# A fused attention, feed-forward and recurrence kernel: roots of the last group norms on ScalarE, an output bias part formed ahead, a third bank for the last receptance, last steps on VectorE, and a rearranged first attention

## The reference

```python
# layer 0
x = x + attention(qkv(layernorm(x)), self_mask) @ w_ao + b_ao          # 16 heads of 16
x = x + attention(q(layernorm(x)), kv(encoder), cross_mask) @ w_co + b_co
x = x + gelu(layernorm(x) @ w1 + b1) @ w2 + b2
# layer 1
xn = layernorm(x); sx = previous_token(xn) - xn
x5 = xn + sx * (maa_stack + tanh((xn + sx * maa_x) @ maa_w1) @ maa_w2)  # five mixes
w = exp(-exp(time_decay + tanh(x5[1] @ decay_w1) @ decay_w2))
r, k, v, g = x5[3] @ Wr.T, x5[0] @ Wk.T, x5[2] @ Wv.T, silu(x5[4] @ Wg.T)
for t: out = r_t . (u * k_t v_t + s); s = k_t v_t + w_t * s             # 32 heads of 8
att = group_norm(out, 32 groups of 8) * gn_w + gn_b
x = x + (att * g) @ Wo.T
xn2 = layernorm(x); sx2 = previous_token(xn2) - xn2
rr = sigmoid((xn2 + sx2 * ffn_maa_r) @ ffn_Wr.T)
kk = relu((xn2 + sx2 * ffn_maa_k) @ ffn_Wk.T) ** 2
x = x + rr * (kk @ ffn_Wv.T)
```

## Time and profile before

| | |
|---|---|
| median of 3 runs | 695.53 us (695.42 to 696.07) |
| profiled execution | 695.38 us, span 693.6 us, mean granted TensorE clock 0.985 |
| TensorE busy | 645.6 us (93%) |
| VectorE busy | 597.0 us (86%) |
| ScalarE busy | 570.5 us (82%) |
| GpSimd busy | 314.9 us (45%) |
| chain that ended last | TensorE 71%, ScalarE 13%, VectorE 8%, issue 5%, GpSimd 2% |

### The profile page before, as it was taken

One profiled execution on the slowest core, in us unless ns is written; L12 is line 12 of the kernel. 1 busy time (PEld: TensorE's weight loads), 2 busy tenths in 40 slices (PEclk: granted clock), 3 DMA queues, 4 the chain that ended last, 5 costly groups with the idle time before them and its releaser, 6 DMA issues.

```text
span 693.6 us, 17394 instructions
## 1 busy us (share of the span) xinstructions
PE 645.6 (93%) x5923; PEld 564.4 (81%) x5923; DVE 597.0 (86%) x1432; ACT 570.5 (82%) x2075; POOL 314.9 (45%) x440
## 2 busy tenths in 40 slices
PE   6778999999999999999999999999999989898876
PEld 5656888788888898898988888888888878787665
DVE  2577668999999999999999999999999996967672
ACT  2579989899999999999999999999999986763311
POOL 1143353555455463626364645455463634441211
PEclk9999999999999999999999999999999999999997
DMA  8920022231405050504122231405050504020200
GB/s 302 329 69 9 1 78 61 62 78 49 98 8 139 1 147 1 144 3 112 35 77 70 62 86 43 104 2 145 1 146 1 139 8 115 24 70 1 69 8 9
DMA packets 53726, 50.45 MB, mean 73 GB/s; under 512 B 6030, under 2 KB 48902, under 8 KB 53254
## 3 DMA queue, kind: packets, MB, share of 16 engines
q1 hardware_dynamic: 53638, 49.34, 25.6%
HBM read 28.62 MB, written 3.93 MB: 47 GB/s over the span
## 4 chain that ended last, share of the span: by engine, by line
PE 71%; ACT 13%; DVE 8%; issue 5%; POOL 2%; DMA 0%; SPq 0%; POOLq 0%; ACTq 0%; DVEq 0%
PE PS_B L542 13%; PE PS_T L637 7%; PE PS_S L542 7%; PE PS_D L549 5%; PE PS_S L618 5%; PE PS_T L645 4%; PE PS_T L549 4%; PE PS_S L549 3%; ACT HG L1240 3%; PE PS_D L783 2%; ACT SC L1199 2%; ACT L1199 2%; PE PS_B L677 2%; PE PS_B L699 2%; ACT PT L1209 2%
## 5 line engine op out<-in xcount | busy, mean ns | idle before, releaser
L1199 ACT ACTIVATE SC<-SC,NMX 128x128 f32<-128x128 f32 x512 | 199.7, 400 | 5.6 <-DVE NMX L934 5.4
L1199 ACT ACTIVATION_READ_ACCUMULATOR SC<-SC,NMX 128x1 f32 x512 | 102.3, 200 | 0.0
L934 DVE TENSOR_REDUCE NMX<-SC 128x4 f32<-128x512 f32 x128 | 85.8, 673 | 0.9 <-POOL SC L1381 0.8
L637 PE MATMUL PS_T<-CST,SC 128*128 128x128 f32 x512 | 79.7, 279 | 5.7 <-ACT SC L1199 2.8
L1209 ACT ACTIVATE PT<-PS_T 128x512 f32<-128x512 f32 x120 | 70.8, 590 | 7.0 <-PE PS_T L637 6.8
L1015 DVE TENSOR_TENSOR_SCAN SS<-W,AJ 128x1024 f32<-128x1024 f32 x32 | 73.1, 2283 | 0.5 <-ACT AJ L1291 0.4
L637 PEld LDWEIGHTS PS_T<-CST,SC 128*128 128x128 f32 x512 | 60.2, 144 | 14.5 <-ACT PT L1209 5.3
L1379 POOL TENSOR_TENSOR SC<-SC,MADD 128x512 f32<-128x512 f32 x48 | 60.2, 1273 | 12.0 <-DVE SC L909 11.9
L542 PE MATMUL PS_B<-MX,W 128*128 128x128 f32 x512 | 62.9, 276 | 0.7 <-ACT KR L1256 0.7
L1381 POOL TENSOR_TENSOR SC<-SC,MADD 128x512 f32<-128x512 f32 x32 | 40.7, 1273 | 48.3 <-DVE SC L909 48.3
L909 DVE TENSOR_TENSOR SC<-PS_S,MASK 128x512 f32<-128x512 f32 x80 | 52.1, 684 | 11.5 <-PE PS_S L618 11.5
(11 more groups left out here) (208 smaller groups left out, 1602.8 us busy)
## 6 DMA issues: line engine op xcount, KB each, us to landing
W<-EW SPq DMA_DIRECT2D x32, 512.0 KB, 4.7
V<-values_by_head SPq DMA_DIRECT2D x28, 512.0 KB, 5.7
W<-in_weights SPq DMA_DIRECT2D x1, 4160.0 KB, 19.6
ENC<-in_enc SPq DMA_DIRECT2D x16, 128.0 KB, 2.4
out<-X SPq DMA_DIRECT2D x16, 128.0 KB, 6.0
X<-in_x SPq DMA_DIRECT2D x1, 1920.0 KB, 15.8
values_by_head<-VC SPq DMA_DIRECT2D x14, 128.0 KB, 1.8
W<-in_weights SPq DMA_DIRECT2D x1, 1280.0 KB, 8.7
```

The source lines that it names most:

```text
L637: last = pe.transpose(PS_T[:, j * T:(j + 1) * T], SC[:, nr(b, a) % 2, g, j, :], ident)
L934: dve.tensor_reduce(NMX[:, nr(b, a) % 2, GH * g:GH * g + GH], SC[:, nr(b, a) % 2, g], AX_X, ALU.max, negate=True)\
L1199: last = act.activation(SC[:, nr(b, a) % 2, g, j, :], SC[:, nr(b, a) % 2, g, j, :], ACT.Exp, bias=NMX[:, nr(b, a) % 2, h:h + 1], accum_out ...
```

## The change

- a_key of the first four attentions (FIRST = 4) is done by VectorE with a multiply-add (new semaphore a_dk); ScalarE's a_key does nothing there.
- The turned value biases move behind the first scores; their projections move ahead of the first transposition of probabilities, together with a matmul by the identity that adds the row. ScalarE copies both results, ahead of its first exponential; VectorE does nothing for them.
- For the last two sequences ScalarE takes the square root of the group norm's variance (d_root_of), VectorE one reciprocal (d_inverse), and the twelve small steps are left out. One-column activations of Exp, Sqrt or Tanh into EARLY are placed at five points of ScalarE's queue.
- For the last sequence: GpSimd forms gate times norm scale and gate times norm bias (d_gates); TensorE multiplies the second by the output weights ahead of time (d_biasout) and adds the main part to it in the bank turns; VectorE multiplies the turned norm directly (d_gated) and d_affine is left out. ScalarE takes the root of the layer norm's variance (d_root) and VectorE the reciprocal. VectorE does d_shift, d_relu2 (relu and square, straight from the bank) and d_final. The receptance goes to the bank values. The state times receptance follows each scan at once.
- All order lists are new, and four entries of KEEP_WARM change: ("b_turn", 0, 15) 3 to 0, ("b_turn", 1, 15) 6 to 1, ("d_turn", 0, 14) 5 to 0, ("d_keyrec", 0, 14) 14 to 0.

The core of the diff (of the order lists, the parts around the first scores and around the decays on ScalarE):

```diff
-    ('a_query', 1, 1): 2, ('b_turn', 0, 15): 3, ('b_turn', 1, 15): 6, ('d_out', 0, 14): 2, ('d_turn', 0, 14): 5,
-    ('d_keyrec', 0, 14): 14, ('d_val', 0, 14): 2, ('d_own', 0, 15): 2, ('d_read', 0, 15): 2,
+    ('a_query', 1, 1): 2, ('b_turn', 0, 15): 0, ('b_turn', 1, 15): 1, ('d_out', 0, 14): 2, ('d_turn', 0, 14): 0,
+    ('d_keyrec', 0, 14): 0, ('d_val', 0, 14): 2, ('d_own', 0, 15): 2, ('d_read', 0, 15): 2,
...
+    ("a_scores", 0, 0), ("b_low2", 0, 3)]
...
+    ("a_exps", (1, 2, 0), 3), ("a_exps", (1, 2, 1), 3), ("a_prob_copy", (1, 0), 3), ("d_first_states", 0, 4),
+    ("d_own", 0, 5), ("a_exps", (1, 3, 0), 3), ("a_prob_copy", (1, 1), 3), ("a_exps", (1, 3, 1), 3),
+    ("d_ocopy", 0, 5), ("a_prob_copy", (1, 2), 3), ("b_decay1", 0, 4), ("a_lessmask", 0, 2), ("a_enc_copy", 0, 2),
+    ("b_decay2", 0, 4), ("d_squares", 0, 5), ("d_root_of", 0, 5), ("b_decays", 0, 4), ("a_prob_copy", (1, 3), 3), ("a_widen", 1, 3),
+    ("a_exps", (0, 0, 0), 1), ("b_keyrec", 0, 4), ("a_exps", (0, 0, 1), 1), ("a_spread", 1, 3), ("a_scale", 1, 2),
+    ("a_val", 1, 2), ("a_exps", (0, 1, 0), 1), ("b_values", 0, 4), ("a_exps", (0, 1, 1), 1), ("a_key", (1, 0), 2),
+    ("b_gatetanh", 0, 4), ("a_key", (1, 1), 2), ("d_affine", 0, 5), ("a_prob_copy", (0, 0), 1),
...
+                if nr(b, a) < FIRST:
+                    pe.wait_ge(a_dk, nr(b, a) + 1)
+                else:
+                    pe.wait_ge(a_k, 2 * (nr(b, a) - FIRST) + 2)
...
+                    for k, name in enumerate(("ao", "co")):
+                        for kt in range(CT):
+                            pe.matmul(PS_D[:, k * C:(k + 1) * C], BVT[:, k, kt, :], w(name, kt, C, 0, C),
+                                      start=(kt == 0), stop=False)
+                        last = pe.matmul(PS_D[:, k * C:(k + 1) * C], ident, row(name), start=False, stop=True)
+                    last.then_inc(set_bo, 1)
...
+            def d_biasout(b, _):
+                if b == B - 1:
+                    pe.wait_ge(d_gws, 1)
+                    pe.wait_ge(d_a, 2 * B)
+                    for kt in range(CT):
+                        pe.matmul(turns, GB[:, kt, :], w("o", kt, C, 0, C), start=(kt == 0), stop=False)
...
+            def a_key(b, a):
+                if nr(b, a) < FIRST:
+                    dve.wait_ge(a_kps, nr(b, a) + 1)
+                    for par in range(2):
+                        for t in range(CT):
+                            last = dve.tensor_scalar(KP[:, par, t, :], keys[:, t * T:(t + 1) * T],
+                                                     CST[:, K_PAR + par:K_PAR + par + 1], KB[:, a, par, t:t + 1],
+                                                     ALU.mult, ALU.add)
+                    last.then_inc(a_dk, 1)
...
+            def d_inverse(b, _):
+                if b >= B - LAST:
+                    dve.wait_ge(d_gsd, b - B + LAST + 1)
+                    dve.reciprocal(GY(b)[:, :], GE[:, :]).then_inc(d_inv, 1)
...
+                    dve.tensor_tensor(YT[:, :, :], tiles(dbank(b)[:, 0:C]), GW[:, :, :], ALU.mult).then_inc(d_yt, 1)
...
+            def d_relu2(b, _):
+                if b == B - 1:
+                    dve.wait_ge(d_kps, 1)
+                    dve.wait_ge(d_fps, b)
+                    dve.wait_ge(d_kk, b)
+                    keys = tiles(dbank(b)[:, 0:C])
+                    dve.tensor_scalar(RL[:, :, :], keys, 0.0, None, ALU.max).then_inc(d_relu, 1)
+                    dve.wait_ge(d_relu, B)
+                    dve.tensor_tensor(KK[:, :, :], RL[:, :, :], RL[:, :, :], ALU.mult).then_inc(d_kk, 1)
...
+                if not later(b, a) and g == 0 and half == 0:
+                    act.wait_ge(set_bv, 1)
+                    act.activation(BVT[:, :, :, :].rearrange("p k t n -> p (k t n)"), PS_D[:, :], ACT.Copy)\
+                        .then_inc(set_bvt, 1)
+                    act.wait_ge(set_bo, 1)
+                    at = ROWS.index("ao"), ROWS.index("co")
+                    for k in range(2):
+                        last = act.activation(ROW[:, at[k], :], PS_D[:, k * C:(k + 1) * C], ACT.Copy)
+                    last.then_inc(set_rows, 1)
...
             def b_low(b, _):
+                if b == B - 1:
+                    act.activation(EARLY[:, 3:4], EW[:, 0, 0:1], ACT.Exp)
...
                 act.activation(EW[:, :, 1:T], DW[:, :, 0:T - 1], ACT.Exp, scale=-1.0).then_inc(b_ew, 1)
+                if b == B - 1:
+                    act.activation(EARLY[:, 4:5], EW[:, 0, 0:1], ACT.Sqrt)
...
                 act.activation(OH[:, :, :], tiles(dbank(b)[:, 0:2 * T]), ACT.Copy).then_inc(d_oh, 1)
+                if b == B - 1:
+                    act.activation(EARLY[:, 5:6], EW[:, 0, 0:1], ACT.Sqrt)
...
+            def d_root_of(b, _):
+                if b >= B - LAST:
+                    act.wait_ge(d_v, b + 1)
+                    act.wait_ge(set_eps, 1)
+                    act.activation(GE[:, :], GV(b)[:, :], ACT.Sqrt, scale=1.0 / RS, bias=EPST[:, 0:1])\
+                        .then_inc(d_gsd, 1)
+                    if b < B - 1:
+                        act.activation(EARLY[:, 1:2], EW[:, 0, 0:1], ACT.Tanh)
+
+            def d_root(b, _):
+                if b == B - 1:
+                    act.wait_ge(d_var, B)
+                    act.activation(D_SD[:, 0:1], D_MV[:, 1:2], ACT.Sqrt, scale=1.0, bias=EPST[:, 0:1]).then_inc(d_sd, 1)
...
                 turned(XM[:, :, 1:T + 1], dbank(b)[:, 0:C], "r2_w", "r2_b").then_inc(d_ln, 1)
+                if b == B - 1:
+                    act.activation(EARLY[:, 2:3], EW[:, 0, 0:1], ACT.Tanh)
...
+            def d_gates(b, _):
+                if b == B - 1:
+                    pool.wait_ge(b_g, B)
+                    pool.wait_ge(set_gnc, 1)
+                    for k, of in enumerate((GW, GB)):
+                        for t in range(CT):
+                            last = pool.tensor_scalar(of[:, t, :], tiles(G[:, :])[:, t], GNC[:, k, t:t + 1], 0.5,
+                                                      ALU.mult, ALU.mult)
+                    last.then_inc(d_gws, 1)
```

202 lines of the change are left out of this document (122 added, 80 removed).

## The result

The changed kernel takes 692.35 us, the median of 5 runs (691.80 to 695.81), against 695.53 for the kernel before (694.26 to 696.07, 5 runs). The ratio is 0.9967 with a 95% interval of 0.9952 to 0.9982: faster by 0.3%, which is 2.3 us by the ratio and 3.2 us by the medians. The forecast was 689.7. The time is inside the range of 684.0 to 694.5, but the gain of 3.2 us is little more than half of the 5.8 forecast, and it is just outside the likeliest case's own 687 to 692. Measured again, beside the experiments, ten runs had a median of 694.97 against 695.81, ratio 0.9991 (0.9976 to 1.0007): there no difference from the kernel before is shown.

A forecast was written before the change was run, and what follows sets the result against it. TensorE was taken to bound the rounds (37.01 of 37.21 us busy), single-step chains the start and the time from 640 us. -2.7 - 0.3 + 3.5 - 6.2 = -5.7, from 695.4 to 689.7 us, range 684.0 to 694.5.

The forecast's parts named there:

- the likeliest case: Whole kernel: the summed terms hold, giving 689.7 us, with its own range of 687 to 692; chance 0.55.
- part 2: Rounds and run-down: rounds stay TensorE-bound, and the receptance-key product leaves its place ahead of the scan, -0.3 us.
- part 3: From 631 us to sequence 15's read-out: table loads delay the copy of keys and receptances, a loss of 3.5 us.
- part 1: The start: keys on VectorE, earlier scaling and a fuller TensorE bring the second sequence's scores earlier, -2.7 us.
- The walk: The start, step by step: scores at about 13.5, first exponential at 19.7, second sequence's scaling at 24.9 us.
- Part 4: The last sequence from its read-out: shorter roots, kept clock and shorter chain steps, -6.2 us, bounds 5 and 7.
- clock and second root: Last sequence: output projection kept at full clock, -1.0 us, and the layer norm's root on ScalarE, -0.35.
- A: From 631 us to sequence 15's read-out: table loads covered or fewer, -2.5 there, 683.7 us; chance 0.12.
- B: The start gives nothing, its gain ending at a later wait such as the input load: 692.4 us; chance 0.14.
- C: Rounds: the new order opens a wait of 0.69 us in each at the scores, 698.0 us; chance 0.09.
- E: Last sequence gives 2.5 us less, by a clock fall or warm-up delaying the transposition: 692.2 us; chance 0.06.
- D: Table switches drain ScalarE as long as a load, four exposed, 5.1 us more: 694.8 us; chance 0.04.

The follow-up runs named there:

- the second profile: The changed kernel measured once more, unchanged, and profiled again: median 694.97 us of 10 runs, profiled execution 693.54 us.
- the restored list: The changed kernel with all four warm-up entries set back to 3, 6, 5 and 14: 693.90 us.

## Why the prediction was right and wrong, point by point

- **What bounds the kernel, and the rounds (part 2): right inside the rounds, wrong at their ends and behind them, +1.4 for -0.3.** 37.20 to 37.24 us a round, 37.21 before, and from the third mark to that of sequence 12 372.2 us for 372.1. But the new orders cost 0.5 us ahead of these rounds and 0.2 behind them, 0.8 in all with what the rounds add, for which the sum had nothing. That is the other step that failed: the new orders were priced at a gain of 0.3, and cost 1.4. In the run-down the forecast -0.3 came out as +0.57, from the new orders (32.75 with the old ones, 33.31 and 33.32 with the new), and 1.6 more in executions whose clock falls at 563 us. No such fall was in the sum; the waits in front of it are only 1.22 and 0.69 us. The -0.3 was read from a row of part 3, at 657.46, where the same 0.33 is booked once more.
- **The start (part 1): 2.0 in the profiled execution and 2.7 in the second profile, for 2.7.** The second sequence's scores began at 33.51 and 32.83 us, where the kernel before had 35.55. The second mark lies 99.72 and 99.18 us behind the first statistics, for 101.87. The new orders then give back 0.8 (above), which leaves the -1.2 of the table; to the mark of sequence 14 it takes 582.3 to 583.0 us without the fall at 563, for 584.2. The walk was not right step by step. The first scores were put at 13.5, since PE would have the keys by 12.0; they came at 14.70. The 16 records of keys and queries took 3.19 us at a granted clock of 1.00, where the kernel before took 1.05 and 1.06 for eight each; 2.15 in the second profile, whose scores came at 13.90. Why they vary was not tried. So the first exponential came at 20.62, no earlier than before, and not at 19.7. From the scores on, the walk holds: the first exponential 5.92 us behind them (6.2 forecast), the values' product at full clock (1.13 us), the scaling 11.0 us behind them (11.4 forecast), and from the scaling to the second scores 1.1 gained for 1.0. All of this stands on one profile of the kernel before. The same start took 101.87 us in it and 103.62 in the kernel with the last sequence's changes alone, by how the clock fell, so the nearness of 2.7 is in part luck.
- **Part 3: the mechanism right, the size wrong, 5.4 for 3.5.** The five loads, the copy more than 2 us behind its matmuls, the idle TensorE and the half clock in the value products are all there, and the experiments show that they are the cause. Counted from the mark of sequence 15, the copy came 3.5 us later (28.98 for 25.51), as forecast to a tenth. From there to the outer product it grew by 1.9 us and not 1.4: the selecting products ran at half clock too (2.85 us for 1.96), and the four warm-up records behind them were still running when the output projection's input came, which cost 0.4. And the gain of 1.4 from the outer product to the read-out became nothing, 12.95 us for 12.98. This is the step that failed here: the prediction took out the 28 warm-up records as something that only held up the mixing, and gave TensorE's clock no term behind them. In the changed kernel the clock falls right there, from 668.9 to 672.4 us, and the receptance product takes 1.92 us. Of the fourteen profiles, the nine without warm-up matmuls ahead of sequence 14's layer norm and keys have a fall between 658 and 673 us, and the five with them have none there (that with the restored list has one earlier, from 649.0 to 655.9). Where the fall comes elsewhere the stretch takes 11.86 us, so 1.1 of the 1.4 was there to be had.
- **Part 4: right, 5.8 for 6.2.** From the read-out to the last value product it takes 14.68 us, where 14.2 was forecast. By its terms: root to norm 1.98 (2.23), norm to output projection 1.06 (1.0), from there to ScalarE's scaling 1.33 (clock and second root, 1.35), from there to the value product 1.00 (1.26), the end 0.44 (0.35). The output projection ran at full clock. Alone in the kernel before it brings 6.3.
- **The rivals.** A, loads covered: no; of the five loads of part 3 none was covered in full, only those of the last sequence were. B's 692.4 is the measured time by luck: in its mechanism the start gives nothing, and it gave 2.0 to 2.7. C: no wait opened in each round. E: no. D: the Trainium skill (ScalarE: Activation LUTs, "What ACT_TABLE_LOAD costs") adds a drain to each switch. By the timeline the load at 647.28 ends at 648.56 and the root begins at 648.58, and the squares end at 647.27, so there is no drain. The same page of the Trainium skill ("Table sets: the hidden batching unit") puts exp and tanh in one set and the root in another. The trace agrees: each change between them shows one load of 1.28 us, and the exponential at 650.29, behind the dummy tanh, shows none.
- **The sum.** -1.2 + 1.6 + 0.6 + 5.4 - 5.8 is, unrounded, +0.4 in the profiled execution, against -5.7. Without the fall at 563 us it would be -1.1. The rest down to the median's -3.2 I put to falls that most of the five runs did not have (three have a clock of 0.990), which their times and the other profiles suggest and no profile of such a run shows. The misses are 1.9 us in part 3, 1.7 by the new orders (0.8 up to the mark of sequence 13 and 0.9 in the run-down), 0.6 in the start and 0.4 in part 4, and the fall of 1.6.

## What to carry to other kernels

Price an operation that needs other tables at the queue behind it, not at its own chain: here a root whose norm was ready 2.4 us sooner held up a copy which another engine waited for, and cost 5.9 us. Where a change opens an idle stretch of TensorE or takes its fillers away, book the clock as a term of its own, at the products behind the gap, and again behind whatever is moved. A new order of the queues that leaves each round as it was can still cost at the first and the last of them (0.8 us here). And measure a large change in parts: the last sequence's part alone was worth more than the whole.

## What the runs showed of the hardware

- The same program, with the same waits to 0.01 us, has its clock fall at a place in one execution and not in another. Those between 560 and 680 us lasted between 3 and 7 us; the one at 563 us cost 1.6 us and the one at 641 us 1.5. Runs of the kernel before show it too: on one chip 694.0 to 694.4 us at a mean granted clock of 0.991 and 0.992, 697.6 to 697.8 at 0.979 and 0.980.
- A table load starts before the inputs of its activation are there: at 647.28, right behind the squares, while VectorE's sums, which the root reads, ended at 647.73. So 0.45 us of it was hidden without any dummy, and a dummy placed ahead of other work only moves the load in front of that work.
- The query and key products of the start took between 2.15 and 3.19 us for the same 16 records at a granted clock of 1.00. Transfers ran in the fastest case as in the slowest (a busy share of the DMA engines of 0.99 and 1.01). What slows them stays open.
